# Last tanh stage of a hybrid network: three one-pass products of split operands in place of a float32 product

## The reference

```python
def _L1_ffn_ref(x, weight, aux_weight1, aux_weight2, bias):
    h = jnp.einsum('btc,cd->btd', x, weight)
    h = jnp.einsum('btc,cd->btd', h, aux_weight1)
    h = jnp.einsum('btc,cd->btd', h, aux_weight2)
    return jnp.tanh(h + bias)
...
x = x + _L1_ffn_ref(_layernorm(x, axis=-1), L1_ffn_weight, L1_ffn_aux_weight1, L1_ffn_aux_weight2, L1_ffn_bias)
```

## Time and profile before

| what | value |
|---|---|
| median of 3 runs | 3836.1 us (3835.32 to 3837.97) |
| the profiled execution, its time | 3835.71 us |
| its span, first to last instruction | 3833.9 us |
| last tanh stage, first to last instruction | 3753.36 to 3833.9 us of the span |
| PE busy over the span | 91% |
| DVE, ACT, POOL busy over the span | 62%, 55%, 38% |
| mean granted TensorE clock | 0.962 of full speed |

### The profile page before, as it was taken

One profiled execution on the slowest core, in us unless ns is written; L12 is line 12 of the kernel. 1 busy time (PEld: TensorE's weight loads), 2 busy tenths in 40 slices (PEclk: granted clock), 3 DMA queues, 4 the chain that ended last, 5 costly groups with the idle time before them and its releaser, 6 DMA issues. The chain is left out here.

```text
span 3833.9 us, 115714 instructions
## 1 busy us (share of the span) xinstructions
PE 3505.2 (91%) x44514; PEld 3084.7 (80%) x44514; DVE 2365.9 (62%) x6483; ACT 2113.1 (55%) x6525; POOL 1465.5 (38%) x2245
## 2 busy tenths in 40 slices
PE   8948999699838999699999999999988999999998
PEld 7838999577728999699899999999976777777777
DVE  6774555588764554544444444444446888888894
ACT  3345555355445555244444444444444888888895
POOL 3444665201024665244444444444444222222215
PEclk9969999799969999899999999999999999999999
DMA  3133443411143443300000000000000000000002
GB/s 121 45 134 97 92 92 75 125 46 51 51 167 98 94 94 71 99 3 3 3 3 3 3 3 3 3 3 3 3 6 16 2 2 2 2 2 2 2 2 93
DMA packets 137901, 164.62 MB, mean 43 GB/s; under 512 B 11392, under 2 KB 127264, under 8 KB 137376
## 3 DMA queue, kind: packets, MB, share of 16 engines
q1 hardware_dynamic: 112800, 123.81, 10.0%
q0 software_dynamic: 24576, 33.57, 5.3%
HBM read 97.18 MB, written 60.16 MB: 41 GB/s over the span
## 5 line engine op out<-in xcount | busy, mean ns | idle before, releaser
L2249 ACT ACTIVATE wa_S<-wa_S,wa_top 128x256 f32<-128x256 f32 x1024 | 511.6, 506 | 138.9 <-DVE wa_top L2313 138.0
L1887 DVE TENSOR_TENSOR so_raw<-so_rows,so_masks 128x1024 f32<-128x1024 f32 x256 | 313.5, 1225 | 228.3 <-PE so_rows L1589 220.7
L2313 DVE CUSTOM_DVE_ANT_0 wa_S<-wa_bank,wa_band 128x256 f32<-128x256 f32 x1024 | 366.9, 420 | 8.4 <-issue 8.2
L1951 POOL TENSOR_TENSOR so_more<-so_compact,so_head 128x384 f32<-128x384 f32 x224 | 185.2, 827 | 337.2 <-PE so_bankC L1671 307.0
L2172 PE MATMUL wa_bank<-ident,wa_S 128*128 128x128 f32 x2048 | 273.9, 275 | 22.2 <-ACT wa_probT L2256 22.2
L2172 PEld LDWEIGHTS wa_bank<-ident,wa_S 128*128 128x128 f32 x2048 | 230.3, 141 | 67.1 <-ACT wa_S L2249 31.2
L1876 DVE SCALAR_TENSOR_TENSOR so_compact<-so_compact,so_bankX 128x96 f32<-128x96 f32 x192 | 48.8, 254 | 363.2 <-PE so_bankX L1707 363.2
L1805 ACT COPY so_O<-so_bankC 128x128 f32<-128x128 f32 x256 | 68.2, 266 | 307.6 <-PE so_bankC L1671 307.5
L1956 POOL TENSOR_TENSOR so_OT<-so_O,so_OT 128x128 fp32r<-128x128 f32 x256 | 117.1, 457 | 307.9 <-ACT so_OT L1811 307.9
L703 ACT ACTIVATE m4e_hT<-m_bank,m4e_bias 128x256 fp32r<-128x256 f32 x256 | 126.3, 493 | 152.2 <-PE m_bank L655 145.0
L703 ACT ACTIVATE m2e_hT<-m_bank,m2e_bias 128x256 fp32r<-128x256 f32 x256 | 126.4, 494 | 149.3 <-PE m_bank L655 142.8
(11 more groups left out here) (450 smaller groups left out, 10201.4 us busy)
## 6 DMA issues: line engine op xcount, KB each, us to landing
m_w_raw<-in_L_ffn_W_dram SPq DMA_DIRECT2D x64, 512.0 KB
sum_dram<-X SPq DMA_DIRECT2D x16, 1024.0 KB, 5.0
X<-sum_dram SPq DMA_DIRECT2D x16, 1024.0 KB, 6.5
X<-in_L_attn_a_x_dram SPq DMA_DIRECT2D x8, 1024.0 KB, 11.8
xn_dram<-m2r_xn SPq DMA_DIRECT2D x16, 512.0 KB, 3.7
sp_gx<-gate_dram SPq DMA_DIRECT2D x64, 128.0 KB, 2.9
xn_dram<-m4r_xn SPq DMA_DIRECT2D x16, 512.0 KB, 3.8
out_dram<-X SPq DMA_DIRECT2D x8, 1024.0 KB, 4.4
```

The costliest lines, as they stand in the source:

```text
L1887: nc.vector.tensor_tensor(AB[:, t % 2].rearrange("p h m t -> p h (m t)"), rows4[:, :, 0:2 * P], masks[:].rearrange("p m t -> p (m t)")[:, ...
L1951: nc.gpsimd.tensor_tensor(state[:, t % UT], compact[:, t % UT, :, None, :].broadcast_to([P, 3, HG, DK]), head[:, None, :, None].broadcast_ ...
L2249: nc.scalar.activation(S[:, n % 2, z], S[:, n % 2, z], ACT.Exp, bias=top[:, n % 2, z:z + 1], scale=-1.0, accum_out=sums[:, i % 2, SET * c ...
L2313: nc.vector.tensor_tensor_reduce(out=S[:, n % 2, z], in0=bS[g][:, eo * SPAN:(eo + 1) * SPAN], in1=band[:], scale=-(D ** -0.5), scalar=3e38 ...
```

## The change

It is made for the call with `out` set only. The weights are loaded to `wc_raw`; ScalarE rounds them to float32r (`wc[:, 0]`, the high part) and VectorE takes the difference (`wc[:, 1]`, the low part). ScalarE's copy of a turned tile now rounds it to float32r. VectorE, in the new `low_xT(i)`, subtracts that high part from the turned tile, still in `psT`, and writes the low part. The product is high x high plus high x low plus low x high: six float32r matmuls to a tile in place of two of float32. `xT_ready`, for which TensorE waits, is now signalled by VectorE's difference.

```diff
+        split = out is not None
+        PARTS = ((0, 0), (0, 1), (1, 0)) if split else ((0, 0),)
+        KIND = F32R if split else F32
+        wc = sb("wc", [P, 2 if split else 1, HC, HID], KIND)
+        wc_raw = sb("wc_raw", [P, HC, HID]) if split else wc[:, 0]
...
+        xT = sb("xT", [P, RING, 2 if split else 1, HC, P], KIND)
...
@@ tensor: products(i)
-                    for c in range(HC):
-                        last = nc.tensor.matmul(psY[i % len(psY)][:, 0:HID], xT[:, i % RING, c, :], wc[:, c, :], start=(c == 0), stop=(c == HC - 1))
+                    steps = [(a, b, c) for a, b in PARTS for c in range(HC)]
+                    for n, (a, b, c) in enumerate(steps):
+                        last = nc.tensor.matmul(psY[i % len(psY)][:, 0:HID], xT[:, i % RING, a, c, :], wc[:, b, c, :],
+                                                start=(n == 0), stop=(n == len(steps) - 1))
                     last.then_inc(psY_ready, 1)
...
-                pe.wait_ge(wc_loaded, 16)
+                if split:
+                    pe.wait_ge(wc_ready, 1)
+                else:
+                    pe.wait_ge(wc_loaded, 16)
@@ scalar
-                    nc.scalar.copy(xT[:, i % RING].rearrange("p c t -> p (c t)"), psT[i % len(psT)][:, 0:HID]).then_inc(xT_ready, 1)
+                    nc.scalar.copy(xT[:, i % RING, 0].rearrange("p c t -> p (c t)"), psT[i % len(psT)][:, 0:HID]
+                                   ).then_inc(xT_high if split else xT_ready, 1)
...
+                if split:
+                    act.wait_ge(wc_loaded, 16)
+                    nc.scalar.copy(wc[:, 0], wc_raw[:]).then_inc(wc_high, 1)
                 for i in range(AHEAD):
                     copy_xT(i)
@@ vector
+                def low_xT(i):
+                    dve.wait_ge(xT_high, i + 1)
+                    high, low = (xT[:, i % RING, part].rearrange("p c t -> p (c t)") for part in range(2))
+                    nc.vector.tensor_tensor(low, psT[i % len(psT)][:, 0:HID], high.bitcast(F32), ALU.subtract).then_inc(xT_ready, 1)
...
+                if split:
+                    dve.wait_ge(wc_high, 1)
+                    nc.vector.tensor_tensor(wc[:, 1], wc_raw[:], wc[:, 0].bitcast(F32), ALU.subtract).then_inc(wc_ready, 1)
+                    for i in range(AHEAD):
+                        low_xT(i)
                 for i in range(NT + 4):
+                    if split and i + AHEAD < NT:
+                        low_xT(i + AHEAD)
                     if i < NT:
                         add_bias(i)
```

More of the change, by code:

```diff
@@ L160, in ps @@
             return ctx.enter_context(nc.psum_tensor(f"{tag}_{name}", shape, dt))
-        wc = sb("wc", [P, HC, HID])
+        split = out is not None
[3 more added lines that the diff above has]
+        wc_raw = sb("wc_raw", [P, HC, HID]) if split else wc[:, 0]
         bias_all = sb("bias_all", [P, HID])
-        xT = sb("xT", [P, RING, HC, P])
+        xT = sb("xT", [P, RING, 2 if split else 1, HC, P], KIND)
         pre = sb("pre", [P, 4, HID])
@@ L174, in tanh_ffn @@
         pre_ready, th_ready, x_ready = sem("pre_ready"), sem("th_ready"), sem("x_ready")
+        wc_high, wc_ready, xT_high = sem("wc_high"), sem("wc_ready"), sem("xT_high")
         with nc.Block() as block:
@@ L178, in _ @@
             def _(sp):
-                sp.dma_start(wc[:], R.centred_dram).then_inc(wc_loaded, 16)
+                sp.dma_start(wc_raw[:] if split else wc_raw, R.centred_dram).then_inc(wc_loaded, 16)
                 sp.dma_start(bias_all[:], bias.rearrange("(a d) -> a d", a=1).broadcast_to([P, HID])).then_inc(bias_loaded, 16)
```

## The result

| kernel | median us | runs (us) | ratio to before, 95% interval |
|---|---|---|---|
| before | 3836.63 | 3835.32 to 3837.97 | |
| after | 3864.59 | 3863.67 to 3865.24 | 1.0075 (1.0063 to 1.0088) |

The change makes the kernel slower by 28.0 us; +31 us was forecast, and the time is inside the stated range. The profiled execution took 3863.99 us, with a span of 3862.1 us.

The account below looks back on a forecast made before the run. The prediction took a closed ring of waits through ScalarE and VectorE, 1.59 us a tile, to set the pace after the change. Ring 29.2, start 1.7 and end 0.1 sum to +31.0 us, giving 3867 us, range 3862 to 3877.

Parts of the forecast that it names:

- The order: Last stage: VectorE's difference ahead of the bias and ScalarE's casts around the tanh form a closed loop once per tile.
- the ring: Last stage: cast, difference, bias, tanh, next cast wait in turn; 1.59 us a tile, +29.2 us; chance 0.76 at full clock.
- rival 2: Last stage: neighbouring operations on one engine do not overlap; 1.82 us a tile, 3880 us, half way 3874; chance 0.10.
- lower end: Last stage: loop from cast to cast, allowing for rounding and a 0.01 shorter difference: 1.57 us a tile, +28.1 us.
- rival 4: Last stage: the loop does not close and TensorE stays the bound; -8.5 us, with the start -6.7, 3829 us; chance 0.04.
- The clock: Last stage: TensorE works 0.94 of 1.59 us a tile and is expected to keep full clock, 2.4 GHz.
- Rival 3: Last stage: TensorE falls to the low clock and is the bound again, up to 1.81 us a tile, 3874 to 3880; chance 0.10.
- Start and end: Last stage: weight rounding and differences delay the fourth tile's turn and tile 5's cast, +1.7 us; last additions +0.1 us.

Follow-up runs that it names:

- Two opposite openings of the ring: Against the changed kernel: bias of tile i ahead of difference of tile i + 4 on VectorE, 3828.92 us; separately, tanh one tile late on ScalarE, 3830.43 us.
- one lengthened link: Changed kernel with VectorE's difference written twice by one instruction, 512 columns instead of 256: 3881.38 us.
- the kernel with the bias first: Changed kernel with two calls exchanged on VectorE, so the bias of tile i precedes the difference of tile i + 4: 3828.92 us.
- Reordering the start: Bias ahead of difference as well; against the changed kernel, three casts precede weight rounding, two differences precede the weights' difference, bias awaited only before use: 3829.19 us.
- the kernel with the float32 product: Changed kernel with two float32 products a tile, nothing rounded or split; VectorE's difference, zero and unread, keeps its place and signals xT_ready: 3865.96 us.

## Why the prediction was right

*The order* was the step that decided, and it held. A sum of loads gives a gain (0.94 us a tile on TensorE, no other engine above it); the order of two queues gives 1.59, and 1.56 was measured. Two opposite openings of the ring gave back 34 to 36 us, one lengthened link came out in full, and the ring alone, without the rest of the change, cost as much as all of it.

*The size of the ring* was off by 0.03 us, or 1.6 us over 58 tiles. The term is the cast, for which I took the copy's 0.37 us: that is what it takes after a wait for the transposes. Directly behind a tanh it takes 0.35, as the copy in the earlier trace rows already did. The bias took 0.47 in place of 0.48, and the handover to ScalarE 0.03 in place of 0.04, which had been read where the tanh also stood behind a copy; the difference until the bias took 0.35 in place of 0.34. The other terms came out as read. Neighbours overlap in the ring too, by 0.07 us on VectorE and 0.09 on ScalarE, though the first of them has just ended a wait, so rival 2 is refuted.

With 1.56 the ring lies just under the lower end that the prediction gave it (1.57), which allowed for rounding and not for a shorter cast. By that lower end the time would have been 3836.1 + 28.1 + 1.8 = 3866 us, and 3864.6 was measured. Of the 3.0 us between +31.0 and +28.0 the ring accounts for 1.6, and start and end for 0.3; the last 1.1 is that the medians differ by less than the stage does (29.1 us), which is within what the seven stages ahead of it vary.

*TensorE.* Six products at 0.12 us each and 0.22 for the transposes, 0.94 us: with the ring open a bias starts every 0.93 us. The forecast of rival 4, 3829 us, is close to what the kernel with the bias first measures, 3828.92. The gain of a faster TensorE was priced nearly rightly; in the changed kernel it could not act. That the two agree to 0.1 us is in part luck: rival 4 has -8.5 us for the tiles and +1.8 for the start, and the stage with the bias first has -9.1, +1.4, and -0.6 at the end.

*The clock.* The granted clock stayed at its upper level (2.4 GHz) through windows in which TensorE was busy for 7.3 of 10 us, with an idle stretch of 0.39 us in each tile; with the wide difference it was busy for 6.24 of 10 us, also at full clock. Rival 3 did not come about. After its rise at the start of the stage (7.6 us in before the change, 7.5 after it) the granted clock was full to the end. The Trainium skill ("TensorE: Matmul & The Clock Gate", section "A second HAM failure mode: psum-queue depth-cycling") reports a kernel with bf16 products of 512 columns in which idle moments between groups make the clock go back and forth. By that pattern the clock here would have been at its lower level for part of the time; no stretch of this stage after its start shows it.

*Start and end.* +1.5 us against +1.7. That TensorE turns the fourth tile only after the differences have begun is in the timeline (idle 3.02 us, ended by the difference). But this wait is not the whole cause. Reordering the start moved the turn 1.0 us ahead of where the changed kernel has it, and the cast of tile 5 only 0.4: 1.1 of the 1.5 us stayed. And the kernel with the float32 product, which does not split the weights, also has its cast of tile 5 after 8.74 us, 1.2 later than in the kernel before. How the start divides between the weights, the bias that VectorE waits for, and the low clock is open. That GpSimd's last five additions stand back to back at the end (3.47 us in place of 5 x 0.72) and that nothing is lost there was right.

## What to carry to other kernels

When an operation is put into an in-order queue, write down the order of both queues it couples and look for a way from one operation back to the next of its kind: if the way leads from each tile to the next, its length can set the pace although no engine is full. The sign of it in this profile is that no engine is full and each of the two waits for the other; a fourth bank did not help, and exchanging two calls on one of the two engines did. An extra pass is better placed behind the operation that others wait for, not ahead of it, when it works for a tile that is needed much later; here that was worth 35.7 us.

## What the runs showed beyond that

A wait of TensorE that the profile puts down to a buffer's release (0.39 us a tile, ended by the bias) stayed at 0.40 us when the buffers were increased from three to four.

The exchange that opens the ring leaves a kernel 0.2% faster than the one before, where the stage itself became 10% shorter (72.2 in place of 80.5 us). Of the 8.3 us, 9.1 come from 58 tiles at 0.929 us in place of 1.086 (3764.60 to 3818.48 us, cast to cast) and 0.6 from the end, where the last additions are closer together (4.6 us in place of 5.2); the start takes 1.4 back.
